# Target indices in two buffers, expert 0's low weight halves on VectorE, and expert 1 described inside expert 0

## What is computed

```python
capacity = max(1, int(CF * N / E))            # 640 rows, N = 4096 tokens, E = 8 experts
probs = softmax(xf @ router_w.T)
topw, topi = top_k(probs, 2)
# the pairs of each expert are ordered by weight, and the first 640 are kept
disp[e, pos] = xf[token]
g = einsum('ecd,edf->ecf', disp, wg)          # 256 -> 1024
u = einsum('ecd,edf->ecf', disp, wu)
eo = einsum('ecf,efd->ecd', silu(g) * u, wd)  # 1024 -> 256
out.at[token].add(eo * weight)
```

## Time and profile before

| | us |
|---|---|
| median of 3 runs | 745.66 |
| lowest, highest | 744.47, 749.24 |
| the profiled execution | 746.98 |
| its span in the trace | 744.6 |
| mean granted clock of TensorE in it | 0.905 |
| TensorE busy | 586.8 (79%) |
| VectorE busy | 479.2 (64%) |
| ScalarE busy | 319.3 (43%) |
| GpSimd busy | 295.1 (40%) |

### The profile page before, as it was taken

How to read it: one execution, slowest core, us unless ns; L and a number is a source line. 1 busy time by engine, 2 the same in 40 slices (tenths; PEclk the granted TensorE clock), 3 DMA queues, 4 the chain that set the end, 5 groups by cost and what they waited for, 6 DMA issues and landing times.

```text
span 744.6 us, 13847 instructions
## 1 busy us (share of the span) xinstructions
PE 586.8 (79%) x4041; PEld 545.8 (73%) x4041; DVE 479.2 (64%) x1306; ACT 319.3 (43%) x717; POOL 295.1 (40%) x440
## 2 busy tenths in 40 slices
PE   3999788998993001699969969969969969969991
PEld 2677677887772001599969959959959959969990
DVE  2688898997777877677537637637636636535531
ACT  4577577875544000255325425324324324434430
POOL 6689757876783700220240240240330330420404
PEclk9999999999996555599989989989989989989996
DMA  4312268535567300252162152252242342430303
GB/s 126 109 64 73 73 200 251 154 111 169 191 190 233 120 1 0 72 156 85 51 141 85 58 134 85 69 121 85 80 111 85 94 96 85 115 76 1 37 0 35
DMA packets 87793, 74.85 MB, mean 101 GB/s; under 512 B 7996, under 2 KB 84166, under 8 KB 87752
## 3 DMA queue, kind: packets, MB, share of 16 engines
q1 hardware_dynamic: 78760, 58.63, 25.7%
q0 software_dynamic: 8992, 15.73, 10.0%
HBM read 52.32 MB, written 22.03 MB: 100 GB/s over the span
## 4 chain that ended last, share of the span: by engine, by line
PE 37%; DVE 22%; issue 12%; POOL 10%; DMA 5%; DVEq 1%; ACT 1%; POOLq 0%; SPq 0%; ACTq 0%
PE bank L1328 21%; PE bank L1340 10%; POOL out L528 6%; DMA out<-yo,s_idx 3%; POOL xg L518 3%; PE bank L1288 2%; DVE feat L844 2%; DVE hit L897 2%; DVE x L863 2%; PE bank L1302 1%; DVE yo L1064 1%; DVE hid L1074 1%; DVE st L865 1%; DVE hid_l L1079 1%; PE bank L1243 1%
## 5 line engine op out<-in xcount | busy, mean ns | idle before, releaser
L1328 PE MATMUL bank<-xT_h,w_h 128*128 128x320 f32 x512 | 164.7, 322 | 42.1 <-DVE hid L1074 40.1
L1328 PE MATMUL bank<-xT_l,w_h 128*128 128x320 f32 x512 | 162.7, 318 | 0.4 <-issue 0.4
L1328 PE MATMUL bank<-xT_h,w_l 128*128 128x320 f32 x512 | 162.4, 317 | 0.0
L518 POOL DMA_INDIRECT xg<-h_rows,g_idx x40 | 42.7, 1068 | 301.6 <-DVE g_idx L1017 291.8
L1328 PEld LDWEIGHTS bank<-xT_h,w_h 128*128 128x128 f32 x512 | 100.2, 196 | 45.8 <-DVE hid L1074 41.8
L672 ACT CAST hid_h<-hid 128x320 fp32r<-128x320 f32 x128 | 58.9, 460 | 136.9 <-DVE hid L1074 132.9
L1074 DVE TENSOR_TENSOR hid<-act_g,bank 128x320 f32<-128x320 f32 x128 | 62.2, 486 | 82.9 <-ACT act_g L668 64.4
L668 ACT ACTIVATE act_g<-bank 128x320 f32<-128x320 f32 x128 | 55.8, 436 | 115.0 <-PE bank L1328 110.2
L1328 PEld LDWEIGHTS bank<-xT_l,w_h 128*128 128x128 f32 x512 | 100.4, 196 | 0.9 <-issue 0.9
L1328 PEld LDWEIGHTS bank<-xT_h,w_l 128*128 128x128 f32 x512 | 100.1, 195 | 0.0
L1340 PE MATMUL bank<-w_h,hid_h 128*128 128x256 f32 x320 | 93.1, 291 | 0.4 <-DVE hid_l L1079 0.4
(11 more groups left out here) (189 smaller groups left out, 1179.4 us busy)
## 6 DMA issues: line engine op xcount, KB each, us to landing
w_raw<-wg SPq DMA_DIRECT2D x32, 256.0 KB, 3.3
w_raw<-wu SPq DMA_DIRECT2D x32, 256.0 KB, 4.4
w_raw<-wd SPq DMA_DIRECT2D x16, 512.0 KB, 6.0
...
```

What stands on the lines that cost most here:

```text
L518: nc.gpsimd.indirect_dma_start(out=xg[par][:, a, :], out_offset=None, in_=h2_rows, in_offset=bass.IndirectOffsetOnAxis(ap=g_idx[par][:, a: ...
L1328: last = MM(bank[2 * h + m][:, 0:HCAP], W[i][:, f, at:at + P], XT[j][:, k, cols], start=n == 0, stop=n == 3 * KC - 1)
```

## The change

**`s_idx` becomes two buffers**, taken by the expert's parity; `find_targets` copies without waiting for `sc_d`, and `scatter` takes the buffer's number.

**The low halves of expert 0's slices 0 to 5** are subtracted by DVE and no longer by POOL: slices 0 to 3 behind `find_tokens(0)` and `place_masks(1)`, slice 4 between the last two `x_low`, slice 5 inside slice 0 of expert 0. The semaphore `sp_l0` goes; SP's load of expert 1's first weights waits for `sp_l`. `place_counts(1)` and `place_slots(1)` stand among the `x_low`.

**Expert 1 is described inside expert 0**: `find_weights(0)`, `describe_tiles(1)`, the facts and the rows in slices 0 and 1, `look(1)` at slice 2, `find_tokens(1)` at slice 3 instead of 1, and expert 1's transposes at slices 5, 6 and 7 instead of 4, 5 and 6. On PE `look(1)` no longer stands ahead of expert 0's first product.

**PE's loop** now runs over experts 1 to 4, as DVE's does, with expert 0 in front and 5, 6 and 7 behind, all written out.

```diff
--- before.py
+++ after.py
@@ -193,7 +193,7 @@
         got = sb("got", [P, NV, CT])
         tok = sb("tok", [P, CT])
         g_idx = [sb(f"g_idx{i}", [P, CT], I32) for i in range(2)]
-        s_idx = sb("s_idx", [P, CT], I32)
+        s_idx = [sb(f"s_idx{i}", [P, CT], I32) for i in range(2)]
         w_sum = sb("w_sum", [P, CT])
         w_slot = [sb(f"w_slot{i}", [P, CT]) for i in range(2)]
 
@@ -295,7 +295,7 @@
         pre_d = sem("pre_d")
         ge_d, in_d, tn_d, ri_d = sem("ge_d"), sem("in_d"), sem("tn_d"), sem("ri_d")
         facts_d, look_d, got_d, fin_l, idx_d = (sem(n) for n in ("facts_d", "look_d", "got_d", "fin_l", "idx_d"))
-        raw_a, raw_b, sp_h, sp_l, sp_l0 = (sem(n) for n in ("raw_a", "raw_b", "sp_h", "sp_l", "sp_l0"))
+        raw_a, raw_b, sp_h, sp_l = (sem(n) for n in ("raw_a", "raw_b", "sp_h", "sp_l"))
         ga_d = [sem(f"ga_d{g}") for g in range(XG)]
         trx_d, xh_d, xl_d = sem("trx_d"), sem("xh_d"), sem("xl_d")
         gu_d, silu_d, hid_d, hh_d, hl_d, dn_d = (sem(n) for n in ("gu_d", "silu_d", "hid_d", "hh_d", "hl_d", "dn_d"))
@@ -385,7 +385,7 @@
                 sp.dma_start(gate_t[b], mod_all[:, b, 3, :].unsqueeze(1).to_broadcast([P, TB, D])).then_inc(st_gate, 16)
 
             sp.wait_ge(sp_h, 4)
-            sp.wait_ge(sp_l0, 4)
+            sp.wait_ge(sp_l, 4)
             load_weights(1, 0, raw_a)
 
             def expert(e, last):
@@ -501,17 +501,6 @@
             nc.gpsimd.tensor_copy(vals[:, :, :, 3], wT(w_mid[:, :, :])).then_inc(r_pool, 1)
             nc.gpsimd.tensor_copy(vals[:, :, :, 4], wT(w_r2[:, :, :])).then_inc(r_pool, 1)
 
-            def split_low(e, f, count):
-
-                raw = raw_a if f < FC // 2 else raw_b
-                wait(pool, raw, (e + 1) * WEIGHT_LOADS * 16)
-                wait(pool, sp_h, count + 1)
-                nc.gpsimd.tensor_tensor(w_l[:, f, :], w_raw[:, f, :], w_h[:, f, :].bitcast(F32), ALU.subtract)\
-                    .then_inc(sp_l0, 1)
-
-            for f in range(FC - 2):
-                split_low(0, f, f)
-
             def gather(e, par):
 
                 for a in range(CT):
@@ -520,13 +509,13 @@
                         in_offset=bass.IndirectOffsetOnAxis(ap=g_idx[par][:, a:a + 1], axis=0))\
                         .then_inc(ga_d[a // 2], 16)
 
-            def scatter(e):
+            def scatter(e, par):
 
                 wait_apart(pool, sc_d, e * CT * 16 + 16, apart)
                 for a in range(CT):
                     wait_apart(pool, ym_d, e * CT + a + 1, apart)
                     nc.gpsimd.indirect_dma_start(
-                        out=out_rows, out_offset=bass.IndirectOffsetOnAxis(ap=s_idx[:, a:a + 1], axis=0),
+                        out=out_rows, out_offset=bass.IndirectOffsetOnAxis(ap=s_idx[par][:, a:a + 1], axis=0),
                         in_=yo[:, a, :], in_offset=None, compute_op=ALU.add).then_inc(sc_d, 16)
 
             for i in range(2):
@@ -542,13 +531,13 @@
                 wait_apart(pool, ym_d, e * CT, apart)
                 wait_apart(pool, idx_d, e + 2, apart)
                 gather(e + 1, 1 - par)
-                scatter(e - 1)
+                scatter(e - 1, 1 - par)
 
             with pool.Fori(0, (E - 2) // 2) as k:
                 expert(k * 2 + 1, 1)
                 expert(k * 2 + 2, 0)
-            scatter(E - 2)
-            scatter(E - 1)
+            scatter(E - 2, 0)
+            scatter(E - 1, 1)
             pool.wait_ge(sc_d, E * CT * 16 + 16)
 
 
@@ -659,6 +648,7 @@
                 x_high(0, 0, g, bk=g)
 
             def expert(e, par, first=False, last=False):
+                xf = FC - XG if first else XF
                 for f in range(FC):
                     for h in range(2):
                         i = e * 2 * FC + 2 * f + h
@@ -670,8 +660,8 @@
                         if f >= 2 or not first:
                             wait(act, dn_d, e * FC + f - 1)
                         nc.scalar.copy(hid_h[f % 2][:, h * HCAP:(h + 1) * HCAP], hid[h][:, :]).then_inc(hh_d, 1)
-                    if not last and XF <= f < XF + XG:
-                        x_high(e + 1, 1 - par, f - XF)
+                    if not last and xf <= f < xf + XG:
+                        x_high(e + 1, 1 - par, f - xf)
                     if f < 2:
 
                         split_high(e, FC - 2 + f, e * FC + FC - 2 + f, implied=True)
@@ -1018,8 +1008,7 @@
 
             def find_targets(e, par):
 
-                wait(dve, sc_d, e * CT * 16 + 16)
-                V.tensor_copy(s_idx[:, :], g_idx[par][:, :])
+                V.tensor_copy(s_idx[par][:, :], g_idx[par][:, :])
 
             def find_weights(e, par):
 
@@ -1027,8 +1016,6 @@
                 dve.wait_ge(ws_l, e + 1)
                 TT(w_slot[par][:, :], w_sum[:, :], got[:, 4, :], ALU.add).then_inc(ws_d, 1)
 
-            dve.sem_inc(sp_l, FC - 2)
-
             def split_low(e, f, count):
 
                 wait(dve, sp_h, count + 1)
@@ -1037,7 +1024,9 @@
             describe(0)
             find_tokens(0, 0)
             place_masks(1)
-            describe(1)
+            for f in range(4):
+                split_low(0, f, f)
+            place_counts(1)
 
             def x_low(e, par, g, bk=7):
                 n = min(2, CT - 2 * g) * P
@@ -1046,11 +1035,11 @@
                 V.tensor_tensor(xT_l[par][:, :, sl], bank[bk][:, 0:2 * n].rearrange("p (c n) -> p c n", c=KC),
                                 xT_h[par][:, :, sl].bitcast(F32), ALU.subtract).then_inc(xl_d, 1)
 
-            for g in range(XG):
-                x_low(0, 0, g, bk=g)
-            find_weights(0, 0)
-            place_counts(1)
+            x_low(0, 0, 0, bk=0)
             place_slots(1)
+            x_low(0, 0, 1, bk=1)
+            split_low(0, 4, 4)
+            x_low(0, 0, 2, bk=2)
 
             def weigh(e, par, lo=0, hi=CT):
 
@@ -1080,22 +1069,39 @@
                                     hid_h[f % 2][:, h * HCAP:(h + 1) * HCAP].bitcast(F32), ALU.subtract)\
                         .then_inc(hl_d, 1)
 
+                def describe_ahead(f):
+                    if f == 2:
+                        describe_tiles(e + 2)
+                    if f in (3, 4):
+                        describe_facts(e + 2, f - 3)
+                    if f == 5:
+                        describe_rows(e + 2, 0)
+
+                xf = FC - XG if first else XF
                 for f in range(FC):
                     hidden(f, 0)
+                    if f == 0 and first:
+                        find_weights(0, 0)
+                        describe_tiles(1)
+                        describe_facts(1, 0)
+                    if f == 1 and first:
+                        describe_rows(1, 1)
+                        describe_rows(1, 2)
                     if f == 0 and not first:
                         weigh(e - 1, 1 - par, 0, 2)
-                    if f == 1 and not last:
+                    if f == (3 if first else 1) and not last:
                         find_tokens(e + 1, 1 - par)
-                    if f == 2 and ahead:
-                        describe_tiles(e + 2)
+                    if ahead:
+                        describe_ahead(f)
                     if f == 3:
                         find_targets(e, par)
-                    if f in (3, 4) and ahead:
-                        describe_facts(e + 2, f - 3)
-                    if f == 5 and ahead:
-                        describe_rows(e + 2, 0)
                     hidden_low(f, 0)
                     hidden(f, 1)
+                    if f == 0 and first:
+                        describe_facts(1, 1)
+                        describe_rows(1, 0)
+                    if f == 1 and first:
+                        describe_rows(1, 3)
                     if f == 0 and not first:
                         weigh(e - 1, 1 - par, 2)
                     if f == 5 and ahead:
@@ -1105,8 +1111,10 @@
                     if f == 7 and not last:
                         find_weights(e + 1, 1 - par)
                     hidden_low(f, 1)
-                    if not last and XF <= f < XF + XG:
-                        x_low(e + 1, 1 - par, f - XF)
+                    if f == 0 and first:
+                        split_low(0, 5, 5)
+                    if not last and xf <= f < xf + XG:
+                        x_low(e + 1, 1 - par, f - xf)
                     if f == 6 and ahead:
                         describe_rows(e + 2, 3)
                     if f < 2:
@@ -1305,11 +1313,8 @@
             look(0)
             pe.wait_ge(r_dve, 5)
             count_masks(1)
-            for g in range(XG - 1):
+            for g in range(XG):
                 transpose_x(0, 0, g, first=True)
-            wait(pe, got_d, 1)
-            look(1)
-            transpose_x(0, 0, XG - 1, first=True)
 
             def gate_up(e, par, f, first=False):
                 W, XT = (w_h, w_l), (xT_h[par], xT_l[par])
@@ -1345,11 +1350,15 @@
                         last.then_inc(y_tile, 1)
                 last.then_inc(dn_d, 1)
 
```

(20 more changed lines are left out.)

## The result

The changed kernel takes 696.39 us (median of 4 runs, 695.6 to 701.46) against 745.97 us of the kernel before (4 runs, 744.47 to 749.24): a ratio of 0.9344 [0.929, 0.9398]. The forecast was 699.0 us, range 692 to 709. The profiled execution took 696.68 us, its span 694.7.

What follows compares the result with a forecast made beforehand. PE waited for DVE's `hid` while DVE waited for scatter DMAs at the `s_idx` copy. From 746.98 us, -48.7 - 4.7 + 0.2 + 2.1 + 2.3 + 1.5 = -47.3 gives 699.7; median forecast 699.0, range 692 to 709.

Steps and rivals of the forecast that it cites:

- Part 1: Expert loop: two `s_idx` buffers end six scatter waits, saving 36.9 us of PE idle and 11.8 of slow matmuls, -48.7.
- The search: Threshold search: three slow steps become plain once POOL's subtractions leave, -4.7 us, bounds 0 and 4.9.
- PE's start: Start of expert 0: gathers beside expert 1's first weight load delay PE by 0.6 us, starting at 309.9, +0.2.
- Slices 0 to 2 with `look(1)`: Expert 0: moved description work and `look(1)` between PE groups cost +2.1 us net, bounds 0.5 and 4.
- `look(2)`'s wait: Expert 0: PE waits once for `x_low(2)` ahead of `look(2)`, +2.3 us, bounds 1.8 and 4.1.
- Fetches: PE's program: six written-out experts instead of four add instruction fetch gaps, +1.5 us, bounds 0 and 5.
- Late `act_g`: Expert loop: five short PE waits for `hid`, about 3.2 us, come from late `act_g`, cause unknown, and stay.
- A: Prologue and first passes cost more: load collides fully, slices 0 to 2 stall, fetches cost 5: about 706; chance 0.13.
- B: The new terms hide and the late `act_g` in the experts goes as well: about 694 us; chance 0.08.
- C: Late `act_g` stops being hidden, costing 2.5 us more in each of six experts: 714 us; chance 0.07.
- D: The scatter wait comes back in full at `weigh` in the experts: time stays near 745 us; chance 0.03.
- E: TensorE does not keep 2.4 GHz over its long run; a quarter at 1.2 GHz gives 791 us; chance 0.03.

Runs made afterwards that it cites:

- e2_gpsimd_splits: The changed kernel with GpSimd again subtracting expert 0's six low halves during the search, expert 1's first load behind POOL's fourth: 697.06 us.
- e3_late_load: The changed kernel, where SP also waits for expert 0's last gather before loading expert 1's first weights: 693.59 us.
- e1_targets_only: The kernel before with only the two `s_idx` buffers and no wait for the scatters: 695.65 us.
- e6_pe_written_out: The changed kernel with PE's loop over experts 1 to 4 written out: 694.96 us (2 runs).
- e11_no_load_wait: e9_parts_1_2 without SP's added wait for the last gather before expert 1's first weight load: 685.92 us.
- e9_parts_1_2: The changed kernel with expert 1 described ahead of expert 0 again, PE's loop over experts 0 to 5, and SP's load waiting for the last gather: 689.23 us.
- e7_act_written_out: The changed kernel with ScalarE's loop over experts 1 to 6 written out: 696.38 us (2 runs).
- e10_act_written_out: e9_parts_1_2 with ScalarE's loop over experts 1 to 6 written out: 686.75 us.

## Why the prediction was right, point by point

**Part 1** (forecast -48.7): right, in mechanism and size. Alone it takes 51.2 us out of the part behind `look(2)` (392.47 to 341.26). Of these, 1.6 are short waits for `hid` (2.6 to 1.0 us behind `look(2)`) and 0.7 `issue` gaps (1.4 to 0.7), which the forecast had kept; 48.9 remain. An expert lasts as forecast: the first gathers of four experts in a row start at 415.07, 461.67, 508.07 and 554.81, which is 46.6, 46.4 and 46.7 us, against the 46.7 named. The terms in the forecast's bracket (eight slices of 5.3, 3.2 and 0.65) make only 46.25, so the agreement to 0.1 us is in part luck.

**The search** (forecast -4.7): right, -4.67: the three slow steps are now 2.24 or 2.25 us. So are all others but three, one of 2.33 and two of 2.73 us, which the kernel before has as well (2.32 and 2.73), so "every search step" said too much. It returns when POOL's subtractions come back (`e2_gpsimd_splits`), so they were the cause.

**PE's start** (forecast +0.2): this term was mis-sized, +2.6. The step that failed is "I take a delay of 0.6". The runs show 2.6 in its place (`e3_late_load`): the gathers' rows came 2.6 and 3.5 us later, at and above the upper bound of 3, and DVE's own chain hid 0.9 of the 3.5, inside the 0.5 to 1.4 named. The time of the load was forecast well: on the clock of the kernel before it is issued at 301.1, as said. What was misread is where this lies in the gathers. In the kernel before their traffic runs from about 299 to 306 us, so 301 is in their first third and not "in the last third" (busy time by stretch in the kernel before; the second number from the right is the DMA engines' share):

```profile
298.00:300.00 2.00, 0.72 (x4) 0.33 (x3) 1.96 (x7) 0.00 (x0) 1.39 (x3) 0.50 0.43 121
300.00:302.00 2.00, 0.00 (x0) 0.00 (x0) 2.00 (x4) 0.00 (x0) 1.70 (x2) 0.50 0.56 166
302.00:304.00 2.00, 1.12 (x4) 0.71 (x4) 0.34 (x2) 0.58 (x1) 1.39 (x2) 0.50 0.72 201
304.00:306.00 2.00, 0.86 (x4) 0.86 (x5) 0.57 (x1) 0.00 (x0) 0.00 (x0) 0.50 0.58 170
```

The first gate/up matmul at 306.17 is 1.0 us off the 305.2 named as the mark, on a shorter attention half.

**Slices 0 to 2 with `look(1)`** (forecast +2.1): about right. The part to `look(2)` grew by 4.1 us against `e1_targets_only` (46.75 - 42.65), of which 2.2 are the wait below: 1.9. But the waits of 0.6 and 0.35 us for `hid` that the forecast laid out for slices 0 and 2 are not in the trace; `look(1)`, 2.11 us at 320.87, accounts for the term alone.

**`look(2)`'s wait** (forecast +2.3): right, 2.18 us once. The forecast's upper bound was that the clock falls in it, and it fell, which cost about 1 us more (the matmuls from 354.90 to 357.7 run at half speed).

**Fetches** (forecast +1.5): mis-sized, 0 in the changed kernel. Its trace has no gap named "issue", and with two more experts written out there is none either. The gap is not bound to the count of first passes: `e1_targets_only`, with PE's loop as before, shows 0.7 us of it and `e2_gpsimd_splits` 0.7 us. That a fetch makes it was argued and is not shown. In `e1_targets_only` the block on queue 8 comes at 376.0 us, beside the gaps, but in `e2_gpsimd_splits` it comes at 385.0, and its gaps are over at 381. And in the changed kernel a block comes at 380.0 while two queues hold 94% and 17% of the 16 engines over half a us, in `e6_pe_written_out` at 428.0 beside 120%, and PE has no `issue` gap in either. The Trainium skill ("Runtime: NRT & Kernel Launch", Instruction fetch mechanics) calls the cost of a block mostly hidden; the traces of the changed kernel and of `e6_pe_written_out` agree.

**Late `act_g`** (forecast kept at 3.2 in five waits): 2.0 us in four waits. The forecast's count was wrong by one: the five short waits before include the 0.62 us at 315.54, which it rightly puts down to `place_slots` elsewhere. The other four make 2.6 us, in experts 2 to 5. In the changed kernel they are in experts 1 to 4. The row in expert 1 shows ScalarE arriving late (without it the same idle time is 1.37 us, in `e11_no_load_wait`), and PE 0.53 us behind:

```profile
378.99 0.44 ACT L658 ACTIVATE act_g<-bank 128x320 f32<-128x320 f32 x1 [4.40 <-PE bank L1333]
```

```profile
380.00 0.41 PE L1333 MATMUL bank<-xT_h,w_h 128*128 128x320 f32 x1 [0.53 <-DVE hid L1063]
```

Four of them make 3.1 us behind `look(2)` (340.59 in `e9_parts_1_2` against 337.51 in `e11_no_load_wait`), 0.8 each, and an expert is longer by as much. PE's waits show only 0.5 of it. Why ScalarE is late stays open. The bytes of the weight loads and the length of SP's program are ruled out. ScalarE's loop is not shown to be a cause: written out, it leaves two of four in `e7_act_written_out` and none in `e10_act_written_out`, but they also went where only PE's code changed (`e6_pe_written_out`) or only the load's time (`e11_no_load_wait`), with ScalarE's loop in place.

**The total.** The forecast for a profiled execution was 699.7 us, and it took 696.68. The errors: the start +2.4 and the clock +1.0, against fetches -1.5, late `act_g` -0.6 and the old `issue` gaps -1.4 (both counted as staying), and the attention half of this execution -1.4. These make -1.5 of the -3.0. Another -0.4 lie outside the span (2.0 us instead of 2.4), and the other 1.1 us I can't place. So the total is closer than its terms: the largest error at the start was hidden by errors of the other sign.

**Rivals.** A had the right place (the load collides in full) and not the right sum, since no fetch cost came. B did not occur: the late `act_g` are four, as before. C, D and E did not occur either: no wait at `weigh` took the stall's place, and the mean clock was 1.00 over 355.8 us.

What the total hid is that the other parts together bring nothing. From the search's start to the end part 1 alone takes 450.8 us and the full change 453.4, by one trace each; the medians don't tell them apart. Part 2 is worth its 4.7 us only if the load does not then meet the gathers, and part 3 costs more than it saves (by the traces of `e3_late_load` and `e9_parts_1_2`). With the load late and part 3 left out the kernel takes 685.92 us, about 1.5% below the full change.
